# Last group of a hypergraph block kernel finished by graphs 0-1, 2 and 3; one store by halves; a shorter variance

## Chip, cores and metric

The kernel runs on one core of one Trainium2 chip. The metric is the device time of one launch in microseconds (us), the median of the runs shown. The engines are TensorE (PE in the profile, its weight loads PEld), VectorE (DVE), ScalarE (ACT), GpSimd (POOL) and SyncE (SP), which issues most of the transfers.

## Reference

64 independent graphs of 128 nodes with 256 features each. Per graph, with H = (adj != 0):

```
w    = adj[0, :]
Dinv = 1 / (H @ w)            Binv = 1 / column sums of H      (0 where the sum is 0)
conv(x, W, b) = Dinv * (H @ (Binv * (H^T @ (x @ W^T)))) + b
h    = relu(conv(x, W1, b1))                  # 128 x 512
h    = (h - mean) * rsqrt(var + 1e-5) * gamma + beta
y    = conv(h, W2, b2) + x                    # 128 x 256
out  = layernorm(x + y)                       # over the 256 features, eps 1e-5
```

## The kernel before

Four graphs make a group, 16 groups (0 to 15; LAST is 15). A = Dinv H Binv H^T is made once per graph and kept transposed (`at_sb`). For a group, in the names of the code:

- u = (A x) transposed, split into two parts `u_hi` and `u_lo` so that TensorE's faster type keeps the precision; v = W1 u in four chunks k of 128 hidden rows; `r_sb` = relu(v + b1) (ScalarE), `r_hi` a rounded copy (GpSimd, L894), `r_lo` the rest (VectorE, L661).
- The squares of r are added over the chunks (`pair_sb`, `q_sb`), turned by TensorE (`turned_q`, L318) and summed by ScalarE with an accumulating activation (L503) into `sum_sq`, one number a node.
- g = r W2 (scaled by gamma, centred) goes into `bank_g` (L301 to L308). `w2_hi` has two more columns than W2, filled with 1.0 (L919), so that column 256 of `bank_g` holds the sum of r. `make_var1` (L631 to L642) makes max(var, 0) + eps from that sum and `sum_sq`, for two graphs (a half) at a time; GpSimd raises it to -0.5 (`inverse_std1`, L870); `read_g` (L652) scales g by it and adds c2.
- y = A g (L325), `make_z` (L687) adds 2 x + b2 (from `xb_sb`, which GpSimd makes, L886), `take_stats2` and `make_var2` make mean and variance of z, GpSimd the power and the shift mean * rstd (`inverse_std2`, L901 and L909), ScalarE normalises in place (`normalise`, L493), SP stores the whole group (512 KB, L203).

Each engine has its own instruction stream, written out by hand, in which it waits on semaphores; nothing reorders it. A loop step i does on TensorE g of group i, v of i+1, y of i, and the preparation of later groups; on VectorE the statistics of group i-1, g of i, the splits of i+1.

The last group has no successor to interleave with. Its residual 2 x + b2 is put into PSUM by TensorE itself (`ident_2` times `xb_sb`, L427, all four graphs in a row), and y is accumulated on top (L431), a half at a time. Statistics are read straight from PSUM (L838). On VectorE its order is: statistics of group 14 graphs 0-1, variance of half 0, statistics of group 14 graphs 2-3, `read_g` half 0, variance of half 1, `make_var2(14)`, `read_g` half 1, then statistics and variance of z by halves. GpSimd does both `inverse_std1`, then `inverse_std2(14)`, then the two halves of `inverse_std2(15)`. ScalarE normalises group 14 and then graphs 0-1 of group 15 (L513, bias `last_shift2`), VectorE graphs 2-3 (L854). Each half is one store of 256 KB by SP.

Of the kernel before, what the change touches and what calls it, by code (L numbers as in the profile page):

```python
# [5 lines left out]
ALU = mybir.AluOpType  # L6
# [5 lines left out]
P = 128  # L12
# [7 lines left out]
def hypergraph_block(nc, x, adj, W1, b1, gamma, beta, W2, b2, out):  # L20
# [13 lines left out]
    with ExitStack() as ctx:  # L34
# [56 lines left out]
        stat1 = sb("stat1", [P, 4, PER])  # L91
# [9 lines left out]
        last_shift2 = sb("last_shift2", [P, PER // 2])  # L101
# [10 lines left out]
        SUM = DOUT  # L112
# [31 lines left out]
        out_ready, last_out_ready = sem("out_ready"), [sem("last_out_low"), sem("last_out_high")]  # L144
        last_shift2_ready = sem("last_shift2_ready")

# [18 lines left out]
        def _(sp):  # L165
# [31 lines left out]
            def store(i, half=None):  # L197
                part, n = graphs(half), len(each(half))
                if half is None:
                    sp.wait_ge(out_ready, i + 1)  # L200
                else:
                    sp.wait_ge(last_out_ready[half], 1)
                sp.dma_start(out_dram[:, i * PER + part.start:i * PER + part.start + n],  # L203
                             z_sb[:, i % 2, part]).then_inc(stored[i % 2], 16)
# [14 lines left out]
            for i in range(G):  # L219
# [9 lines left out]
                if i >= 1:  # L229
                    store(i - 1)  # L230
            for half in range(2):
                store(LAST, half)
            sp.wait_ge(stored[0], 16 * (G // 2))
            sp.wait_ge(stored[1], 16 * (G // 2) + 16)

        @block.tensor
        def _(pe):
# [57 lines left out]
            def make_g(i, n):  # L295
# [14 lines left out]
                if n % 2:  # L310
                    mm.then_inc(g_made, 1)

# [107 lines left out]
            for n in range(PER):  # L420
                if n < 2:
                    pe.wait_ge(z_ready, LAST * 2 - 1 + n)
                elif n == 2:
                    pe.wait_ge(at_ready, G)
                else:
                    pe.wait_ge(q_summed, G * 2)
                pe.matmul(last_z[n], ident_2[:, :], xb_sb[:, 1, n], start=True, stop=False)  # L427
            for half in range(2):
                pe.wait_ge(g_ready, LAST * 2 + half + 1)
                for n in each(half):  # L430
                    mm = pe.matmul(last_z[n], at_sb[:, LAST % 3, n], g_sb[:, n], start=False, stop=True)  # L431
                mm.then_inc(y_made, 1)

        @block.scalar
        def _(act):
# [54 lines left out]
            def normalise(i, half):  # L490
# [4 lines left out]
                if half:  # L495
                    ins.then_inc(out_ready, 1)

            def sum_q(i):
# [3 lines left out]
                for n in range(PER):  # L502
                    ins = nc.scalar.activation(scratch[:, n], turned_q[:, graph(n)], ACT.Copy,  # L503
# [4 lines left out]
            def normalise_last():  # L508

                act.wait_ge(last_shift2_ready, 1)  # L510
                act.wait_ge(stored[1], landed(LAST - 2, 2))
                for n in each(0):
                    ins = nc.scalar.activation(z_sb[:, 1, n], last_z[n], ACT.Identity,  # L513
                                               bias=last_shift2[:, n:n + 1], scale=rstd2[:, 1, n:n + 1])
                ins.then_inc(last_out_ready[0], 1)
# [75 lines left out]
        def _(dve):  # L591
# [387 lines left out]
```

## Time and profile before

| | us |
|---|---|
| median of 3 runs | 289.74 (289.73 to 290.66) |
| the profiled execution, its own time | 290.7 |
| its span in the trace | 288.9 |
| TensorE busy | 277.7 (96% of the span) |
| VectorE busy | 227.9 (79%) |
| ScalarE busy | 195.6 (68%) |
| GpSimd busy | 138.6 (48%) |

Times inside the kernel are counted from the span's start. The engines run side by side, so a busy share alone doesn't tell what sets the end; the chain of waits follows the work back from the last instruction. A busy time of TensorE contains the draining of its pipeline, so that consecutive matmuls overlap in the rows.

### The profile page before, as it was taken

Reading aid. Unit: us, or ns where it says so; the run is one execution under the profiler, and the core shown is the slowest. Engines: PE = TensorE matmul, PEld = TensorE weight load, DVE = VectorE, ACT = ScalarE, POOL = GpSimd, SP = SyncE. Lnnn points to the kernel's source line nnn. Section 1 sums busy time; section 2 is a strip of 40 time slices with the busy share of each in tenths; the row PEclk is TensorE's granted clock in tenths of the full one; section 3 lists DMA queues with packets and bytes.
Section 4 is the critical chain, followed back from the end, with each engine's and each line's share of the span. In section 5 each row is a group of like instructions: output and inputs, shape, how many; then the busy total and the mean of one; then the engine's idle time right before and its main releaser. Section 6 shows DMA issues by size and latency. Waiting matters only on the chain.

```text
span 288.9 us, 5778 instructions
## 1 busy us (share of the span) xinstructions
PE 277.7 (96%) x1814; PEld 249.0 (86%) x1814; DVE 227.9 (79%) x660; ACT 195.6 (68%) x556; POOL 138.6 (48%) x193
## 2 busy tenths in 40 slices
PE   6899999999999999999999999999999999999991
PEld 6779979898898989899898989899898989889880
DVE  1676579787979888797978888797988879596884
ACT  3288977766767876676677877676678775583614
POOL 2224463637364563636374463636365364536362
PEclk9999999999999999999999999999999999999998
DMA  7920140433513434431433533333423322120104
GB/s 218 309 79 19 40 127 16 112 113 63 173 41 122 113 94 115 122 114 54 152 70 93 140 99 109 100 104 53 136 50 91 97 88 75 36 73 2 50 25 145
DMA packets 37255, 27.70 MB, mean 96 GB/s; under 512 B 10013, under 2 KB 35305, under 8 KB 37225
## 3 DMA queue, kind: packets, MB, share of 16 engines
q1 hardware_dynamic: 37120, 27.30, 33.3%
q8 instruction: 14, 0.23, 0.3%
q14 instruction: 17, 0.13, 0.2%
q10 hardware_dynamic: 104, 0.04, 0.1%
HBM read 17.21 MB, written 8.42 MB: 89 GB/s over the span
## 4 chain that ended last, share of the span: by engine, by line
PE 85%; DVE 7%; issue 2%; POOL 2%; DMA 2%; ACT 1%; DVEq 0%; SPq 0%; POOLq 0%
PE bank_v L291 29%; PE bank_g L308 10%; PE bank_g L301 10%; PE bank_g L303 10%; PE bank_v L325 9%; PE bank_v L276 9%; PE bank_s L255 5%; PE bank_g L318 2%; DMA w_raw<-in_L_gnn_W_dram 2%; POOL rstd L870 1%; DVE g_sb L652 1%; DVE r_lo L661 1%; DVE pair_sb L666 1%; PE bank_g L333 1%; PE bank_g L353 1%
## 5 line engine op out<-in xcount | busy, mean ns | idle before, releaser
L886 POOL TENSOR_TENSOR xb_sb<-x_sb,b_half 128x512 f32<-128x512 f32 (+1 forms) x31 | 41.2, 1331 | 75.6 <-DVE r_lo L661 51.6
L481 ACT ACTIVATE r_sb<-bank_v,vec 128x512 f32<-128x512 f32 x64 | 44.2, 691 | 36.4 <-PE bank_v L291 35.7
L301 PE MATMUL bank_g<-w_hi,r_hi 128*128 128x258 f32 x256 | 65.5, 288 | 0.0
L303 PE MATMUL bank_g<-w_lo,r_hi 128*128 128x256 f32 x256 | 63.8, 282 | 0.0
L894 POOL TENSOR_SCALAR r_hi<-r_sb 128x512 fp32r<-128x512 f32 x64 | 47.9, 749 | 32.4 <-ACT r_sb L481 32.3
L661 DVE TENSOR_TENSOR r_lo<-r_sb,r_hi 128x512 fp32r<-128x512 f32 x64 | 44.7, 719 | 11.1 <-POOL r_hi L894 11.1
L291 PE MATMUL bank_v<-u_hi,w_hi 128*128 128x512 f32 x128 | 50.7, 396 | 0.4 <-DVE u_lo L625 0.4
L291 PE MATMUL bank_v<-u_hi,w_lo 128*128 128x512 f32 x128 | 50.8, 397 | 0.0
L291 PE MATMUL bank_v<-u_lo,w_hi 128*128 128x512 f32 x128 | 50.6, 395 | 0.0
L301 PEld LDWEIGHTS bank_g<-w_hi,r_hi 128*128 128x128 f32 x256 | 48.3, 189 | 1.4
L303 PEld LDWEIGHTS bank_g<-w_lo,r_hi 128*128 128x128 f32 x256 | 48.1, 188 | 1.2
L488 ACT ACTIVATE sq_sb<-r_sb 128x512 f32<-128x512 f32 x64 | 40.2, 634 | 1.9
L308 PE MATMUL bank_g<-w_hi,r_lo 128*128 128x258 f32 x256 | 41.3, 283 | 0.0
L475 ACT ACTIVATE u_hi<-bank_v 128x512 fp32r<-128x512 f32 x32 | 19.1, 598 | 27.0 <-PE bank_v L276 27.0
L493 ACT ACTIVATE z_sb<-z_sb,shift,rstd 128x256 f32<-128x256 f32 x60 | 32.3, 587 | 5.3 <-POOL shift L909 5.3
L308 PEld LDWEIGHTS bank_g<-w_hi,r_lo 128*128 128x128 f32 x256 | 35.2, 189 | 0.0
L870 POOL TENSOR_TENSOR rstd<-stat,half_power 128x2 f32<-128x2 f32 x32 | 22.7, 708 | 24.7 <-DVE stat L642 24.7
L652 DVE SCALAR_TENSOR_TENSOR g_sb<-bank_g,rstd,c 128x256 f32<-128x256 f32 x64 | 28.1, 481 | 8.0 <-POOL rstd L870 8.0
L276 PE MATMUL bank_v<-at_sb,x_sb 128*128 128x128 f32 x256 | 31.4, 276 | 0.7 <-ACT at_sb L469 0.7
L325 PE MATMUL bank_v<-g_sb,at_sb 128*128 128x256 f32 x120 | 31.9, 388 | 0.1
L276 PEld LDWEIGHTS bank_v<-at_sb,x_sb 128*128 128x128 f32 x256 | 29.8, 192 | 1.4 <-ACT at_sb L469 0.9
L325 PEld LDWEIGHTS bank_v<-g_sb,at_sb 128*128 128x128 f32 x120 | 21.4, 189 | 8.6 <-issue 5.3
(99 smaller groups left out, 449.1 us busy)
## 6 DMA issues: line engine op xcount, KB each, us to landing
x_sb<-in_x_dram SPq DMA_DIRECT2D x16, 512.0 KB, 3.8
out_dram<-z_sb SPq DMA_DIRECT2D x15, 512.0 KB, 3.2
adj_sb<-in_adj_dram SPq DMA_DIRECT2D x16, 256.0 KB, 4.0
d_row<-d_rows SPq DMA_DIRECT2D x13, 256.0 KB, 3.4
w_raw<-in_L_gnn_W_dram SPq DMA_DIRECT2D x2, 512.0 KB, 5.9
out_dram<-z_sb SPq DMA_DIRECT2D x2, 256.0 KB, 2.6
turned_h<-h_sb SPq DMA_TRANSPOSE x13, 2.4
d_rows<-dinv SPq DMA_DIRECT2D x13, 2.0 KB, 2.1
```

Of the source, the lines that this page charges most:

```text
L276: mm = pe.matmul(bank_v[:, c, graph(n)], x_sb[:, j % 3, n, graph(c)], at_sb[:, j % 3, n], start=True, stop=True)
L291: mm = pe.matmul(bank_v[:, k % 2], w[:, c, graph(k)], u[:, c], start=(m == 0), stop=(m == len(terms) - 1))
L301: pe.matmul(bank_g[:, n, 0:W2COLS], r_hi[:, i % 2, k, graph(n)], w2_hi[:, k], start=(k == 0), stop=False)
L303: pe.matmul(bank_g[:, n, 0:DOUT], r_hi[:, i % 2, k, graph(n)], w2_lo[:, k], start=False, stop=False, skip_group_check=True)
L308: mm = pe.matmul(bank_g[:, n, 0:W2COLS], r_lo[:, i % 2, k, graph(n)], w2_hi[:, k], start=False, stop=(k == KH - 1))
L325: mm = pe.matmul(bank_v[:, half, (n % 2) * DOUT:(n % 2 + 1) * DOUT], at_sb[:, i % 3, n], g_sb[:, n], start=True, stop=True)
L481: nc.scalar.activation(r_sb[:, k], bank_v[:, k % 2], ACT.Relu, bias=vec[:, k:k + 1]).then_inc(relu_ready, 1)
L488: nc.scalar.activation(sq_sb[:, k], r_sb[:, k], ACT.Square).then_inc(sq_ready, 1)
L493: ins = nc.scalar.activation(z_sb[:, i % 2, n], z_sb[:, i % 2, n], ACT.Identity, bias=shift2[:, n:n + 1], scale=rstd2[:, 0, n:n + 1])
L661: nc.vector.tensor_tensor(r_lo[:, i % 2, k], r_sb[:, k], r_hi[:, i % 2, k].bitcast(F32), ALU.subtract).then_inc(r_lo_ready, 1)
L886: nc.gpsimd.tensor_tensor(xb_sb[:, i % 2, part], x_sb[:, i % 3, part], b2_half[:, :].unsqueeze(1).to_broadcast([P, n, DOUT]), ALU.add).the ...
L894: nc.gpsimd.tensor_scalar(r_hi[:, i % 2, k], r_sb[:, k], 1.0, 1.0, ALU.mult, ALU.mult).then_inc(r_hi_ready, 1)
```

## The change

Five things are edited.

1. *Variance in three operations.* The two extra columns of `w2_hi` hold 1/512 and -1/512, so `bank_g` holds mean and -mean. ScalarE's sum of q is scaled by 1/512. For each graph one scalar_tensor_tensor makes mean * (-mean) + E[r^2], its scalar operand read from PSUM, and one tensor_scalar for the half does max and + eps. The wait for `q_summed` now stands ahead of the first operation. This holds in every group.
2. *Group 14 stored by halves:* ScalarE reports the first half (`half_out_ready`), and SP stores it before it waits for the second.
3. *Half 1 of group 15 graph by graph:* variance, power (GpSimd, one column each), `read_g` and y have signals of their own for graphs 2 and 3.
4. *Order in the last group.* VectorE: both statistics of group 14, variance of half 0, `make_var2(14)`, variance of graph 2, `read_g` half 0, variance of graph 3, `read_g` of 2 and of 3. GpSimd: `inverse_std1` of half 0, `inverse_std2(14)`, then the powers of graphs 2 and 3. TensorE: residual products of graphs 0-1, y of 0-1, residual products of 2-3, y of 2, y of 3.
5. *The last normalisation.* ScalarE does graphs 0-1 and then 2 (GpSimd makes the shift for both halves); VectorE does graph 3 alone. SP stores graphs 0-1 (256 KB) and graph 3 (128 KB); graph 2 (128 KB) is stored by a transfer that ScalarE issues itself.

```diff
+            sp.wait_ge(half_out_ready, 1)
+            store(LAST - 1, graphs(0))
+            sp.wait_ge(out_ready, LAST)
+            store(LAST - 1, graphs(1))
+            sp.wait_ge(last_out_ready[0], 1)
+            store(LAST, graphs(0))
+            sp.wait_ge(last_out_ready[2], 1)
+            store(LAST, slice(3, 4))
...
             for half in range(2):
-                pe.wait_ge(g_ready, LAST * 2 + half + 1)
                 for n in each(half):
+                    if n < 2:
+                        pe.wait_ge(z_ready, LAST * 2 - 1 + n)
+                    elif n == 2:
+                        pe.wait_ge(at_ready, G)
+                    else:
+                        pe.wait_ge(q_summed, G * 2)
+                    pe.matmul(last_z[n], ident_2[:, :], xb_sb[:, 1, n], start=True, stop=False)
+                for n in each(half):
+                    if half:
+                        pe.wait_ge(last_g_ready, n - 1)
+                    else:
+                        pe.wait_ge(g_ready, LAST * 2 + 1)
                     mm = pe.matmul(last_z[n], at_sb[:, LAST % 3, n], g_sb[:, n], start=False, stop=True)
...
-                    ins = nc.scalar.activation(scratch[:, n], turned_q[:, graph(n)], ACT.Copy,
+                    ins = nc.scalar.activation(scratch[:, n], turned_q[:, graph(n)], ACT.Copy, scale=1.0 / HID,
...
+                for part, graphs_done in enumerate((each(0), [2])):
+                    act.wait_ge(last_shift2_ready, part + 1)
+                    for n in graphs_done:
+                        ins = nc.scalar.activation(z_sb[:, 1, n], last_z[n], ACT.Identity,
+                                                   bias=last_shift2[:, n:n + 1], scale=rstd2[:, 1, n:n + 1])
+                    ins.then_inc(last_out_ready[part], 1)
+                act.wait_ge(last_out_ready[1], 1)
+                act.dma_start(out_dram[:, LAST * PER + 2:LAST * PER + 3], z_sb[:, 1, 2:3]).then_inc(stored[1], 16)
...
-                nc.vector.tensor_scalar(stat1[:, 0, part], bank_g[:, part, SUM], 1.0 / HID, None,
-                                        ALU.mult).then_inc(stat1_step, 1)
-                dve.wait_ge(stat1_step, done * 3 + 1)
-                nc.vector.tensor_tensor(stat1[:, 1, part], stat1[:, 0, part], stat1[:, 0, part],
-                                        ALU.mult).then_inc(stat1_step, 1)
                 dve.wait_ge(q_summed, done + 1)
-                dve.wait_ge(stat1_step, done * 3 + 2)
-                nc.vector.scalar_tensor_tensor(out=stat1[:, 2, part], in0=sum_sq[:, part], scalar=1.0 / HID,
-                                               in1=stat1[:, 1, part], op0=ALU.mult,
-                                               op1=ALU.subtract).then_inc(stat1_step, 1)
+                for n in each(half):
+                    ins = nc.vector.scalar_tensor_tensor(out=stat1[:, 0, n:n + 1], in0=bank_g[:, n, MEAN:MEAN + 1],
+                                                         scalar=bank_g[:, n, MEAN + 1:MEAN + 2],
+                                                         in1=sum_sq[:, n:n + 1], op0=ALU.mult, op1=ALU.add)
...
+            def make_last_var1(n):
+                dve.wait_ge(last_g_made if n == 2 else g_made, 1 if n == 2 else G * 2)
+                dve.wait_ge(q_summed, G * 2)
+                nc.vector.scalar_tensor_tensor(out=stat1[:, 0, n:n + 1], in0=bank_g[:, n, MEAN:MEAN + 1],
+                                               scalar=bank_g[:, n, MEAN + 1:MEAN + 2], in1=sum_sq[:, n:n + 1],
+                                               op0=ALU.mult, op1=ALU.add).then_inc(last_step, 1)
+                dve.wait_ge(last_step, n - 1)
+                nc.vector.tensor_scalar(stat1[:, 1, n:n + 1], stat1[:, 0, n:n + 1], 0.0, EPS, ALU.max,
+                                        ALU.add).then_inc(last_var1, 1)
+
+            def read_last_g(n):
+                dve.wait_ge(last_rstd1, n - 1)
+                nc.vector.scalar_tensor_tensor(out=g_sb[:, n], in0=bank_g[:, n, 0:DOUT], scalar=rstd1[:, n:n + 1],
+                                               in1=c2[:, :], op0=ALU.mult, op1=ALU.add).then_inc(last_g_ready, 1)
...
+            take_stats2(LAST - 1, 0)
+            take_stats2(LAST - 1, 1)
             make_var1(LAST, 0)
-            take_stats2(LAST - 1, 1)
+            make_var2(LAST - 1)
+            make_last_var1(2)
             read_g(LAST, 0)
-            make_var1(LAST, 1)
-            make_var2(LAST - 1)
-            read_g(LAST, 1)
-            take_last_stats2(0)
-            make_var2(LAST, 0)
-            take_last_stats2(1)
-            make_var2(LAST, 1)
+            make_last_var1(3)
+            read_last_g(2)
+            read_last_g(3)
+            for half in range(2):
+                take_last_stats2(half)
+                make_var2(LAST, half)
...
-            nc.gpsimd.memset(w2_hi[:, :, DOUT:W2COLS].bitcast(F32), 1.0)
+            for n, mean in enumerate((1.0 / HID, -1.0 / HID)):
+                nc.gpsimd.memset(w2_hi[:, :, DOUT + n:DOUT + n + 1].bitcast(F32), mean)
...
-            for half in range(2):
-                inverse_std1(LAST, half)
+            inverse_std1(LAST, 0)
             inverse_std2(LAST - 1)
+            for n in each(1):
+                pool.wait_ge(last_var1, n - 1)
+                nc.gpsimd.tensor_tensor(rstd1[:, n:n + 1], stat1[:, 1, n:n + 1], half_power[:, n:n + 1],
+                                        ALU.pow).then_inc(last_rstd1, 1)
```

## Rows read from the trace of the kernel before

**Rows 1.** Stretches: length, busy us (instructions) per engine, granted clock, DMA share, GB/s

```profile
200.00:250.00 50.00, 49.98 (x331) 45.08 (x330) 41.39 (x119) 33.48 (x91) 25.77 (x35) 1.00 0.30 85
```

**Rows 2.** Chain that ended last, in order of time: start, us, what

```profile
274.13 1.28 DVE z_sb L687 x2
...
284.16 0.71 POOL rstd L901
...
284.96 0.54 DVE z_sb L854
```

**Rows 3.** VectorE's timeline in the last group: start, us, operation, idle before

```profile
275.33 0.74 DVE L695 BATCH_NORM_STATS2 bn_sb<-z_sb 128x6 f32<-128x256 f32 x2
275.99 0.14 DVE L631 TENSOR_SCALAR stat<-bank_g 128x2 f32<-128x2 f32 x1
276.17 0.64 DVE L634 TENSOR_TENSOR stat<-stat 128x2 f32<-128x2 f32 x1
...
280.67 0.88 DVE L652 SCALAR_TENSOR_TENSOR g_sb<-bank_g,rstd,c 128x256 f32<-128x256 f32 x2 [0.32 <-POOL rstd L870]
281.46 0.75 DVE L838 BATCH_NORM_STATS2 bn_sb<-bank_v 128x6 f32<-128x256 f32 x2
...
282.52 0.17 DVE L708 TENSOR_SCALAR mean<-mv_sb 128x2 f32<-128x2 f32 x1
282.60 0.16 DVE L709 TENSOR_SCALAR var<-mv_sb 128x2 f32<-128x2 f32 x1
282.76 0.76 DVE L838 BATCH_NORM_STATS2 bn_sb<-bank_s 128x6 f32<-128x256 f32 x2
```

**Rows 4.** GpSimd's timeline in the last group

```profile
274.39 2.40 POOL L886 TENSOR_TENSOR xb_sb<-x_sb,b_half 128x1024 f32<-128x1024 f32 x1 [2.64 <-DVE q_sb L673]
...
279.87 0.70 POOL L870 TENSOR_TENSOR rstd<-stat,half_power 128x2 f32<-128x2 f32 x1 [1.80 <-DVE stat L642]
280.53 1.01 POOL L901 TENSOR_TENSOR rstd<-var,half_power 128x4 f32<-128x4 f32 x1
281.62 0.20 POOL L909 TENSOR_TENSOR shift<-mean,rstd 128x4 f32<-128x4 f32 x1
```

**Rows 5.** TensorE's timeline in the last group

```profile
279.00 1.03 PE L427 MATMUL bank_s<-xb_sb,ident 128*128 128x256 f32 x4
...
281.60 1.13 PE L431 MATMUL bank_s<-g_sb,at_sb 128*128 128x256 f32 x4 [0.70 <-DVE g_sb L652]
```

**Rows 6.** ScalarE's timeline in the last group

```profile
281.85 2.07 ACT L493 ACTIVATE z_sb<-z_sb,shift,rstd 128x256 f32<-128x256 f32 x4 [5.30 <-POOL shift L909]
```

**Rows 7.** SyncE's queue, first issue to the end of the last

```profile
283.95 2.41 SPq L203 DMA_DIRECT2D out_dram<-z_sb  x3
```

**Rows 8.** Stretches at the end, columns as in the first group

```profile
287.75:288.00 0.25, 0.00 (x0) 0.00 (x0) 0.00 (x0) 0.00 (x0) 0.00 (x0) 0.50 0.71 246
```

**Rows 9.** DMA issues in the last 3 us: size, us to landing

```profile
out_dram<-z_sb SPq DMA_DIRECT2D x1, 256.0 KB, 2.4
```

**Rows 10.** DMA issues of the whole run, ScalarE's queue

```profile
edge_rows<-in_adj_dram ACTq DMA_DIRECT2D x1, 32.0 KB, 3.2
```

**Rows 11.** VectorE's timeline in group 14's second half

```profile
267.33 0.16 DVE L631 TENSOR_SCALAR stat<-bank_g 128x2 f32<-128x2 f32 x1 [1.47 <-PE bank_g L308]
...
267.80 0.16 DVE L638 SCALAR_TENSOR_TENSOR stat<-sum_sq,stat 128x2 f32<-128x2 f32 x1
267.99 0.17 DVE L642 TENSOR_SCALAR stat<-stat 128x2 f32<-128x2 f32 x1
...
269.85 0.82 DVE L661 TENSOR_TENSOR r_lo<-r_sb,r_hi 128x512 fp32r<-128x512 f32 x1
```

**Rows 12.** GpSimd's timeline in group 14's second half

```profile
269.51 0.63 POOL L894 TENSOR_SCALAR r_hi<-r_sb 128x512 fp32r<-128x512 f32 x1 [0.55 <-ACT r_sb L481]
...
270.90 0.85 POOL L894 TENSOR_SCALAR r_hi<-r_sb 128x512 fp32r<-128x512 f32 x1 [0.76 <-ACT r_sb L481]
```

**Rows 13.** TensorE's timeline, first use of the fourth chunk in group 15

```profile
272.61 0.28 PE L301 MATMUL bank_g<-w_hi,r_hi 128*128 128x258 f32 x1
```

More of the change, by code:

```diff
@@ L195, in load_d, with store @@
                     [P, P * PER])).then_inc(d_row_in[j % 2], 16)
[L197 to L203, printed above, removed]
+            def store(i, part=slice(0, PER)):
+                sp.dma_start(out_dram[:, i * PER + part.start:i * PER + part.stop],
                              z_sb[:, i % 2, part]).then_inc(stored[i % 2], 16)
@@ L228, in _ @@
                     load_x(i + 3)
-                if i >= 1:
+                if 1 <= i < LAST:
+                    sp.wait_ge(out_ready, i)
                     store(i - 1)
-            for half in range(2):
-                store(LAST, half)
-            sp.wait_ge(stored[0], 16 * (G // 2))
-            sp.wait_ge(stored[1], 16 * (G // 2) + 16)
+            sp.wait_ge(half_out_ready, 1)
[6 more added lines that the diff above has]
+            store(LAST, slice(3, 4))
+            sp.wait_ge(stored[0], 16 * (G // 2) + 16)
+            sp.wait_ge(stored[1], 16 * (G // 2) + 32)
         @block.tensor
@@ L311, in make_g @@
                     mm.then_inc(g_made, 1)
+                elif i == LAST and n == 2:
+                    mm.then_inc(last_g_made, 1)
             def turn_q(i):
@@ L419, in _ @@
             pe.wait_ge(xb_ready, G * 2)
[L420 to L427, printed above, removed]
             for half in range(2):
-                pe.wait_ge(g_ready, LAST * 2 + half + 1)
                 for n in each(half):
+                    if n < 2:
[10 more added lines that the diff above has]
+                        pe.wait_ge(g_ready, LAST * 2 + 1)
                     mm = pe.matmul(last_z[n], at_sb[:, LAST % 3, n], g_sb[:, n], start=False, stop=True)
-                mm.then_inc(y_made, 1)
+                    if half:
+                        mm.then_inc(last_y_made, 1)
+                if half == 0:
+                    mm.then_inc(y_made, 1)
         @block.scalar
@@ L496, in normalise @@
                     ins.then_inc(out_ready, 1)
+                elif i == LAST - 1:
+                    ins.then_inc(half_out_ready, 1)
             def sum_q(i):
@@ L845, in _ @@
-            make_var2(LAST - 1)
-            read_g(LAST, 1)
-            take_last_stats2(0)
-            make_var2(LAST, 0)
-            take_last_stats2(1)
-            make_var2(LAST, 1)
+            make_last_var1(3)
[4 more added lines that the diff above has]
+                make_var2(LAST, half)
             dve.wait_ge(stored[1], landed(LAST - 2, 2))
             dve.wait_ge(rstd2_ready, G + 1)
-            for n in each(1):
-                ins = nc.vector.tensor_scalar(z_sb[:, 1, n], last_z[n], mean2[:, 1, n:n + 1],
-                                              rstd2[:, 1, n:n + 1], ALU.add, ALU.mult)
@@ L856, in _ @@
-            ins.then_inc(last_out_ready[1], 1)
+            nc.vector.tensor_scalar(z_sb[:, 1, 3], last_z[3], mean2[:, 1, 3:4], rstd2[:, 1, 3:4], ALU.add,
+                                    ALU.mult).then_inc(last_out_ready[2], 1)
         @block.gpsimd
@@ L869, in inverse_std1 @@
                 pool.wait_ge(var1_ready, i * 2 + half + 1)
-                nc.gpsimd.tensor_tensor(rstd1[:, part], stat1[:, 3, part], half_power[:, part],
+                nc.gpsimd.tensor_tensor(rstd1[:, part], stat1[:, 1, part], half_power[:, part],
                                         ALU.pow).then_inc(rstd1_ready, 1)
@@ L903, in inverse_std2 @@
                 pool.wait_ge(rstd2_ready, done + 1)
-                if half == 0:
-                    nc.gpsimd.tensor_tensor(last_shift2[:, :], mean2[:, 1, part], rstd2[:, 1, part],
+                if half is not None:
+                    nc.gpsimd.tensor_tensor(last_shift2[:, part], mean2[:, 1, part], rstd2[:, 1, part],
                                             ALU.mult).then_inc(last_shift2_ready, 1)
-                if half is not None:
                     return
```

26 lines of the change are left out of this document (12 added, 14 removed).

## Prediction

> **What bounds the kernel now.** I read the table of stretches first. Over 200 to 250 us TensorE is busy 49.98 of 50 us at a granted clock of 1.00 [rows 1], so the loop over groups is TensorE's. VectorE has 8.6 us idle in the same stretch, and nothing that only shortens VectorE's share of a loop step can shorten the step. Nearly the whole change lies behind the loop, in the last 15 us.
>
> I read the chain of waits next. From 274.13 on it has no TensorE piece: it goes over VectorE's z of group 14, statistics, the small variance operations, GpSimd's power, g, statistics, power, and the last normalisation [rows 2]. Then I went down each engine's timeline over the last 14 us [rows 3 to 7]: VectorE and GpSimd hand the work to and fro, and every other engine waits for them. The table of stretches at the end shows the DMA engines 71% busy between 287.75 and 288.00 at 246 GB/s [rows 8]: a full rate of 246 / 0.71 = 346 GB/s, and the last bytes leave at about 287.93. Three stores (512 + 256 + 256 KB = 1.05 MB) at that rate take 3.03 us, so they began at 284.90, 0.95 after group 14's store was issued at 283.95. The last store was issued at 283.95 + 2.41 - 0.37 = 285.99 [rows 7] and took 2.4 us to land [rows 9], so 288.39: 0.46 after its last byte, and 0.5 before the span's end. The end is thus set by the compute chain and, to a smaller part, by a backlog of stores.
>
> **The variance in three operations.** Before, a half takes four dependent operations, in group 14's second half from 267.33 to 267.99 + 0.17 = 268.16, 0.83 [rows 11]. After, two scalar_tensor_tensors that don't wait for each other (0.08 apart, as the two rows of mean and variance at 282.52 and 282.60 show for independent small operations [rows 3]) and one tensor_scalar 0.19 behind (267.80 to 267.99 [rows 11]), 0.17 long: 0.44. That is 0.39 us less in each half. In the loop it is covered by TensorE and I cost it at nothing. Could it leak into the end through group 14? Behind it VectorE runs dense, but its r_lo at 269.85 takes 0.82, with GpSimd's r_hi running since 269.51, where z at 274.13, also over 512 columns, takes 0.64 [rows 2, 11, 12]; 0.39 earlier VectorE would be at 269.46, in a dead heat with it, and the two would only swap places, since GpSimd waits there for ScalarE and that for TensorE. I take 0, with 0.2 of gain as the other end. The scalar operand now comes from PSUM: no row shows that. The nearest are a small operation reading PSUM (0.14 at 275.99) [rows 3] and one reading only SBUF (0.16 at 267.80) [rows 11]; I take 0.16, with 0.1 more each as the upper end, 0.2 in all on the path. ScalarE's factor in the sum of q rides in an operation that exists: 0. The second memset on GpSimd, some 0.1 us, lies in the set-up while GpSimd waits for ScalarE: 0.
>
> **Group 15's first half.** Before, two statistics of group 14 (275.33) end with the next start at 275.99, so 0.66 a pair; then the squaring at 276.17 takes 0.64 instead of some 0.16, until 276.81, which is where GpSimd's add of b2 ends (274.39 + 2.40 = 276.79) [rows 3, 4]. The variance of group 15's first half then still needs two operations. After, both pairs come first: 275.33 + 0.66 + 0.66 = 276.65. Then 0.08, 0.19 and 0.17: ready at 277.09, the power 0.08 later, 277.17 to 277.88 (0.71 [rows 2]). Before, the squaring's end at 276.81 with the 0.17 and 0.19 of two more operations, 0.08 between each, puts it at about 277.4; so it comes some 0.2 earlier although a pair of statistics was moved ahead of it. The squaring, two SBUF inputs, is gone; the new operation reads PSUM, PSUM and SBUF, like z at 274.13 (both in 1.28), which ran beside the same add [rows 2]. If it is held up until 276.79 anyway, 0.14 is lost.
> The Trainium skill ("SBUF — State Buffer", Who interferes with whom) says that a VectorE instruction with two SBUF inputs contends with a GpSimd instruction that reads SBUF, and one with a single SBUF input doesn't; by that rule the 0.14 doesn't arise, and the trace's 0.64 agrees with it.
>
> **The order behind it.** make_var2(14), moved ahead of read_g, starts at 277.00. For two graphs such a block takes 0.56 behind the statistics (282.76 + 0.76 to 284.16 - 0.08 [rows 2, 3]); two more aggregates of 0.16 at most make 0.88 at most, so 277.88 or sooner, when GpSimd comes free. It starts a waiting power 0.04 before the end of the one before (279.87 + 0.70, 280.53 [rows 4]), so that of group 14 runs 277.84 to 278.85 (1.01), the shift 278.93 to 279.13 (0.08 and 0.20, as 281.54 to 281.82 before) [rows 4]. It was ready at 281.82 before. Queued behind both is now the power of graph 2; its variance is wanted only by 279.09 and is ready long before, since on TensorE graph 3's g and two residual pairs still come behind graph 2's g, and the second of these pairs starts at 279.00 [rows 5]. A power of one column isn't in the trace: two columns take 0.71, four 1.01, so 0.15 a column and 0.56 for one; bounds 0.20 (the shift) and 0.71. With starts 0.04 before an end as above: graph 2 279.09 to 279.65, graph 3 279.61 to 280.17 (its variance is ready at 279.2, after read_g of graphs 0 and 1, 277.99 to 278.87). VectorE's g of graph 3 starts 0.10 later (280.57 to 280.67 before [rows 3, 4]), at 280.27. Before, a pair started at 280.67 and the statistics 0.79 later, 0.40 a graph; now one graph is left, and they start at 280.67, not 281.46.
>
> **TensorE's products.** Before, the residual products of graphs 2 and 3 start at 279.00 and take 1.03 [rows 5]. After, y of graphs 0 and 1 takes that place (its g is ready at 278.87) and ends at 280.03. The residuals of 2 and 3 come then, 1.03 at most (a next pair may start before the last has drained), to 281.06, and y of 2 and 3 in 1.13 as before (281.60), to 282.19 at the latest, graph 2 by 281.7. Statistics of graph 0 want 280.03 and start at 280.67, those of graph 2 are due at 281.89 and of graph 3 at 282.27: the work hides all of it, the last by 0.08 at the worst.
>
> **The end.** Statistics to the variance's start: 281.46 to 282.60, then 0.08: the second pair starts at 280.67 + 1.22 = 281.89. Before it had to wait for y until 282.73 (281.60 + 1.13 [rows 5]). From its start to the power is 1.40 (282.76 to 284.16 [rows 2, 3]): 283.29, end 284.00 (0.71). VectorE normalises graph 3 0.80 after the power's start, as 284.16 to 284.96 [rows 2], at 284.09, and is done in 0.54: 284.63, store issued at 284.67. ScalarE normalises graph 2 after the new shift (0.08 + 0.20) and 0.03 more (281.82 to 281.85 [rows 4, 6]), at 284.31; one graph takes 2.07 less three times 0.5, 0.57: 284.88; its own DMA is issued 0.04 later, at 284.92. ScalarE is free: group 14's four run from 279.16 to 281.23 (2.07 [rows 6]), the first half's two from 283.05 to 284.07.
> Group 14's stores are issued at about 280.3 and 281.3 and have left before 283.1. Group 15's: 256 KB issued at 284.10, then 128 KB at 284.67 and 128 KB at 284.92. Together 524 kB at 346 GB/s from 285.05: 286.57, and 0.46 to landing: 287.03. Alone, the last one would land at 284.92 + 0.95 + 0.38 + 0.46 = 286.71, so the backlog still sets it, by 0.32. Landing was at 288.39: **1.36 us gained**. Of this, 1.07 is the last issue (285.99 to 284.92), 0.29 the smaller backlog.
> ScalarE's queue is unused from the start until then. Its only larger transfer took 3.2 us for 32 KB, while SP's queue was loading [rows 10]. The nearest row is SP's last store, so I take the sum above; with 3.2 it lands at 288.12 and 1.1 of the gain is gone.
> The Trainium skill ("DMA: Bandwidth & Descriptors", Where the ~2 µs actually goes) speaks against cutting a store: each pays about 2.0 us fixed, mostly for the receipt. By it the last piece lands near 284.92 + 2.0 + 0.3 = 287.2, and the sum would be 1.2. This trace's 0.95 ahead of the bytes and 0.46 behind make 1.41 instead.
>
> **The sum.** The profiled execution spans 288.9 and took 290.7, 1.8 outside the span; I leave those alone. 290.7 - 1.36 = 289.3, or -0.47%. The median of three runs is 289.74, 0.96 below the profiled one; the same difference gives 288.4. About 0.5% (1.45 us) is what a measurement of this kernel can tell from no change, and the sum lies just under it.
>
> **The rivals.**
> *More than the sum:* the 0.39 does leak through group 14, or the one-column power is nearer 0.45. For it: after 269.5 VectorE is dense. Against: the tie with GpSimd's r_hi [rows 12]. Another 0.2: 288.2.
> *The new small operations are dear:* a power of one column costs 0.71 as two do (0.30 over the two), PSUM scalars 0.2. All on the path: gain 0.9, 288.85.
> *ScalarE's queue is slow to wake:* 3.2 us to landing [rows 10]; gain 0.27, 289.5, no change. For it: the only row of that queue. Against: those engines were full with SP's loads.
> *Slower:* VectorE's earlier instructions in the loop take the memory access from GpSimd before r_hi of the fourth chunk. It ends at 271.75 (270.90 + 0.85) and TensorE first wants it at 272.61 [rows 12, 13], so it has 0.86 to spare. A single VectorE operation (0.64) in its way costs nothing; from 0.86 on it decides, and two in its way cost about 0.4 in each of 14 groups, 5.6 us less 1.4: 294. Against: VectorE moves by 0.39 only, and GpSimd's turn still comes when ScalarE releases it.
>
> **How the numbers follow.** The forecast has 0.62, with its own range 288.0 to 288.8 (0.15 lost at the start, 0.15 a power, 0.2 either way for joints between engines). More than the sum 0.14, dear operations 0.08, the sleeping queue 0.10, slower 0.06. Two in ten left out over both ends: 287.9 to 289.4. Faster by over 0.5% means below 288.29: nearly all of the first rival and 0.28 of the forecast's 0.62, 0.41. Slower by over 0.5%: 0.06. Within: 0.53.
>
> **What the profile after would show.** The step right: first power of group 15 at 277.2, its one-column powers 0.56 long, g of graph 3 at 280.3, second statistics at 281.9, last store issued at 284.9 by ScalarE's queue, landing at 287.0; loop steps unchanged at TensorE. Wrong, if the loop's TensorE idles, if one-column powers take 0.7, if scalar_tensor_tensor with a PSUM scalar is over 0.25, or if ScalarE's store takes over 2.4 us to land.

## The result and the profile after

The changed kernel takes 288.02 us (median of 4 runs, 288.00 to 288.05) against 289.74: a ratio of 0.9933, 95% interval 0.9914 to 0.9952, 1.72 us. The forecast was 1.36 us, with "within 0.5%" as the likeliest outcome (0.53). The profiled executions stand 2.65 us apart (290.7 and 288.05; spans 288.9 and 286.2), because that of before lies about 0.95 above the kernel's median; the first experiment accounts for this.

The last group after the change, from VectorE's timeline:

```profile
274.00 1.40 DVE L709 BATCH_NORM_STATS2 bn_sb<-z_sb 128x6 f32<-128x256 f32 x4
275.31 0.34 DVE L651 SCALAR_TENSOR_TENSOR stat<-bank_g,sum_sq 128x1 f32<-128x1 f32 x2
275.69 0.17 DVE L656 TENSOR_SCALAR stat<-stat 128x2 f32<-128x2 f32 x1
...
277.10 0.88 DVE L666 SCALAR_TENSOR_TENSOR g_sb<-bank_g,rstd,c 128x256 f32<-128x256 f32 x2 [0.36 <-issue]
...
278.43 1.02 DVE L857 SCALAR_TENSOR_TENSOR g_sb<-bank_g,rstd,c 128x256 f32<-128x256 f32 x2
279.36 0.75 DVE L867 BATCH_NORM_STATS2 bn_sb<-bank_v 128x6 f32<-128x256 f32 x2
...
280.58 0.78 DVE L867 BATCH_NORM_STATS2 bn_sb<-bank_s 128x6 f32<-128x256 f32 x2
...
282.80 0.54 DVE L884 TENSOR_SCALAR z_sb<-bank_s,mean,rstd 128x256 f32<-128x256 f32 x1 [0.89 <-POOL rstd L930]
```

GpSimd's timeline in the same stretch:

```profile
275.93 0.71 POOL L899 TENSOR_TENSOR rstd<-stat,half_power 128x2 f32<-128x2 f32 x1 [0.48 <-DVE stat L656]
276.61 1.01 POOL L930 TENSOR_TENSOR rstd<-var,half_power 128x4 f32<-128x4 f32 x1
277.70 0.20 POOL L937 TENSOR_TENSOR shift<-mean,rstd 128x4 f32<-128x4 f32 x1
277.85 1.08 POOL L985 TENSOR_TENSOR rstd<-stat,half_power 128x1 f32<-128x1 f32 x2
...
281.99 0.70 POOL L930 TENSOR_TENSOR rstd<-var,half_power 128x2 f32<-128x2 f32 x1 [0.27 <-DVE var L723]
```

TensorE's timeline, and then ScalarE's with its own store:

```profile
276.83 1.02 PE L435 MATMUL bank_v<-xb_sb,ident 128*128 128x256 f32 x4
278.03 1.13 PE L441 MATMUL bank_v<-g_sb,at_sb 128*128 128x256 f32 x4 [0.18 <-DVE g_sb L666]
279.00 1.03 PE L435 MATMUL bank_s<-xb_sb,ident 128*128 128x256 f32 x4
279.86 1.03 PE L441 MATMUL bank_s<-g_sb,at_sb 128*128 128x256 f32 x4
```

```profile
283.00 0.56 ACT L529 ACTIVATE z_sb<-bank_s,last_shift,rstd 128x256 f32<-128x256 f32 x1 [0.16 <-POOL last_shift L934]
283.59 0.39 ACTq L533 DMA_DIRECT2D out_dram<-z_sb  x1
```

The DMA issues of the last 8 us, with the time to landing:

```profile
out_dram<-z_sb SPq DMA_DIRECT2D x3, 256.0 KB, 2.2
out_dram<-z_sb SPq DMA_DIRECT2D x1, 128.0 KB, 2.0
out_dram<-z_sb ACTq DMA_DIRECT2D x1, 128.0 KB, 2.2
```

The first residual product marks the end of the loop in both traces. In the kernel before it starts at 278.14, the 0.86 of one pair ahead of the 279.00 of [rows 5]; in the changed kernel it starts at 276.83. So the work up to that point came 1.31 earlier, and 1.31 has to be added to a time of the changed kernel to compare it with the prediction's:

| step | predicted | measured + 1.31 |
|---|---|---|
| first power of group 15 | 277.17 | 277.24 |
| end of the one-column powers | 280.17 | 280.24 |
| statistics of graph 0 | 280.67 | 280.67 |
| statistics of graph 2 | 281.89 | 281.89 |
| last power | 283.29 | 283.30 |
| graph 3 normalised from | 284.09 | 284.11 |
| ScalarE's store issued | 284.92 | 284.90 |
| end of the span | 287.54 | 287.5 |

In these terms the sum behind the loop holds to 0.1 us. What it lacks lies ahead of the first residual product. TensorE starts y of the first half of groups 0, 1 and 2 at 40.11, 56.91 and 73.32 in the kernel before, steps of 16.80 and 16.41, and at 39.19, 55.57 and 71.98 in the changed kernel, steps of 16.38 and 16.41. One step, that from group 0 to group 1, is 0.42 shorter; all later ones up to group 14 are equal to 0.01. A table in the trace of the kernel before points at the cause. It lists which engine waited for whom (us in total, times, longest); these are TensorE's weight loads:

```profile
PEld bank_s L431 <- DVE g_sb L652: 1.1, 1, 1.1
PEld bank_v L325 <- DVE g_sb L652: 0.5, 1, 0.5
```

The first line is the last group. The second is y of group 0, second half: once in the run, TensorE waits for VectorE's g inside the loop. After the change that line is gone.

### The profile page after: what moved, and what is told of

The parts are those of the page before. It is cut to its first block, busy times and chain, and to the rows that moved or that the text cites. A ratio compares the mean times of both kernels' runs of the same rounds, so it can differ in the third digit from the quotient of the medians.

```text
span 286.2 us, 5751 instructions
## 1 busy us (share of the span) xinstructions
PE 275.8 (96%) x1814; PEld 247.5 (86%) x1814; DVE 227.0 (79%) x628; ACT 196.1 (69%) x557; POOL 136.0 (47%) x196
## 4 chain that ended last, share of the span: by engine, by line
PE 89%; DVE 5%; POOL 2%; issue 2%; ACT 1%; POOLq 0%; DVEq 0%
PE bank_v L296 30%; PE bank_g L313 10%; PE bank_g L306 10%; PE bank_g L308 10%; PE bank_v L332 10%; PE bank_v L281 9%; PE bank_s L260 5%; PE bank_g L325 2%; PE bank_s L365 1%; DVE pair_sb L680 1%; DVE r_lo L675 1%; PE bank_g L360 1%; POOL rstd L930 1%; PE bank_s L267 1%; DVE bn_sb L867 1%
## 5 line engine op out<-in xcount | busy, mean ns | idle before, releaser
L923 POOL TENSOR_SCALAR r_hi<-r_sb 128x512 fp32r<-128x512 f32 x64 | 44.8, 699 | 41.3 <-ACT r_sb L494 41.3
L675 DVE TENSOR_TENSOR r_lo<-r_sb,r_hi 128x512 fp32r<-128x512 f32 x64 | 48.4, 776 | 11.3 <-POOL r_hi L923 11.3
L666 DVE SCALAR_TENSOR_TENSOR g_sb<-bank_g,rstd,c 128x256 f32<-128x256 f32 x62 | 27.1, 478 | 7.3 <-POOL rstd L899 6.9
L899 POOL TENSOR_TENSOR rstd<-stat,half_power 128x2 f32<-128x2 f32 x31 | 21.9, 708 | 17.4 <-DVE stat L656 17.3
L296 PEld LDWEIGHTS bank_v<-u_lo,w_hi 128*128 128x128 f32 x128 | 24.0, 188 | 5.5
```

The lines of the kernel that those rows point to most:

```text
L296: mm = pe.matmul(bank_v[:, k % 2], w[:, c, graph(k)], u[:, c], start=(m == 0), stop=(m == len(terms) - 1))
L675: nc.vector.tensor_tensor(r_lo[:, i % 2, k], r_sb[:, k], r_hi[:, i % 2, k].bitcast(F32), ALU.subtract).then_inc(r_lo_ready, 1)
L923: nc.gpsimd.tensor_scalar(r_hi[:, i % 2, k], r_sb[:, k], 1.0, 1.0, ALU.mult, ALU.mult).then_inc(r_hi_ready, 1)
```

## Experiments

All times are medians, and the ratios are against the kernel before, which was run beside them and gave 289.71 to 289.74.

**1. The kernel before once more.** No edit.

> The kernel before, unchanged, for a second profile. The theory: 0.94 us of the two shown spans (288.9 and 286.2) is no work of the change but of the one profiled execution of before, whose W1 transposes and first S products ran at 0.43 us a matmul where after shows 0.28; this profile should show about 0.28, a span of 288.0, and still a wait of TensorE of 0.4 to 0.5 for g of group 0's second half (the line that makes y waits for VectorE's g). The rival, that the shorter set-up belongs to the change: the W1 transposes take 0.43 again and the span is 288.9.

289.74 us (one run), span 287.9. TensorE's transposes of W1 in the trace behind the recorded rows, and then in this one (min/median/max ns, first and last start):

```profile
L333 PE MATMUL bank_g<-ident,w_raw x8: 421/421/475, 6.0 to 7.6; 128*128 128x128 f32 x8
```

```profile
L333 PE MATMUL bank_g<-ident,w_raw x8: 272/273/331, 6.4 to 7.2; 128*128 128x128 f32 x8
```

W1 arrived later here (6.4), and yet u of group 0 starts at 12.04 and not at 12.96: 0.92 us of the difference between the two profiled executions was one execution's set-up and belongs to no edit. The other 0.4 of the 1.31 is still there between this kernel and the changed one (y of groups 0 and 1 at 39.18 and 55.97, a step of 16.79), and so does TensorE's wait for g.

Group 0 around it, VectorE's timeline of this kernel and then of the changed one:

```profile
35.67 0.88 DVE L652 SCALAR_TENSOR_TENSOR g_sb<-bank_g,rstd,c 128x256 f32<-128x256 f32 x2 [0.92 <-POOL rstd L870]
...
37.40 0.15 DVE L631 TENSOR_SCALAR stat<-bank_g 128x2 f32<-128x2 f32 x1
37.59 0.38 DVE L634 TENSOR_TENSOR stat<-stat 128x2 f32<-128x2 f32 x1
38.08 0.16 DVE L638 SCALAR_TENSOR_TENSOR stat<-sum_sq,stat 128x2 f32<-128x2 f32 x1
38.28 0.17 DVE L642 TENSOR_SCALAR stat<-stat 128x2 f32<-128x2 f32 x1
39.35 0.88 DVE L652 SCALAR_TENSOR_TENSOR g_sb<-bank_g,rstd,c 128x256 f32<-128x256 f32 x2 [0.90 <-POOL rstd L870]
```

```profile
35.44 0.88 DVE L666 SCALAR_TENSOR_TENSOR g_sb<-bank_g,rstd,c 128x256 f32<-128x256 f32 x2 [0.91 <-POOL rstd L899]
...
37.17 0.35 DVE L651 SCALAR_TENSOR_TENSOR stat<-bank_g,sum_sq 128x1 f32<-128x1 f32 x2
37.55 0.21 DVE L656 TENSOR_SCALAR stat<-stat 128x2 f32<-128x2 f32 x1
38.66 0.88 DVE L666 SCALAR_TENSOR_TENSOR g_sb<-bank_g,rstd,c 128x256 f32<-128x256 f32 x2 [0.90 <-POOL rstd L899]
```

Up to 33.9 VectorE runs alike in both. The first half's shorter variance brings g forward by 0.23, the second's by another 0.46, of which 0.2 is the squaring: 0.38 long here instead of 0.16, while GpSimd's r_hi ran from 37.04 to 37.97. TensorE, which starts y of the first half at 39.18 and needs 0.86 for it, could begin the second at 40.04 and begins at 40.28; S behind it then starts 0.34 and u 0.41 later than in the changed kernel.

**2. The shorter variance alone, in all groups.** The kernel before with the first part of the change (columns, scaled sum and operations as there); order, split and stores stay.

```diff
-                nc.vector.tensor_scalar(stat1[:, 0, part], bank_g[:, part, SUM], 1.0 / HID, None,
-                                        ALU.mult).then_inc(stat1_step, 1)
...
+                for n in each(half):
+                    ins = nc.vector.scalar_tensor_tensor(out=stat1[:, 0, n:n + 1], in0=bank_g[:, n, MEAN:MEAN + 1],
+                                                         scalar=bank_g[:, n, MEAN + 1:MEAN + 2],
+                                                         in1=sum_sq[:, n:n + 1], op0=ALU.mult, op1=ALU.add)
```

> Before, with only the three-operation variance (all groups, with the scaled columns and the scaled sum). Theory A: TensorE's wait in group 0 goes (0.42 us), and in the last group the first power comes 0.7 earlier, of which about 0.6 reaches the end because the residual products then hold y of the first half until 280.9: 1.0 us faster than before, 288.7. Rival B, the recorded forecast (the shorter variance is worth nothing in the loop, 0.2 at the start of the end): 289.5. The steps of the loop from group 1 on keep 16.41 us by either.

288.76 us, ratio 0.9967 [0.9947, 0.9986]: 0.98 faster. The step from group 0 to 1 is 16.38, as in the changed kernel. In the last group, VectorE's and TensorE's timelines show the second part; the first residual product is at 278.13, so the times can be held against before as they are:

```profile
276.14 0.35 DVE L633 SCALAR_TENSOR_TENSOR stat<-bank_g,sum_sq 128x1 f32<-128x1 f32 x2
...
279.92 0.88 DVE L648 SCALAR_TENSOR_TENSOR g_sb<-bank_g,rstd,c 128x256 f32<-128x256 f32 x2
280.92 0.76 DVE L834 BATCH_NORM_STATS2 bn_sb<-bank_v 128x6 f32<-128x256 f32 x2
```

```profile
279.86 1.03 PE L431 MATMUL bank_v<-g_sb,at_sb 128*128 128x256 f32 x4
```

The first power of the group starts 0.47 earlier (276.88 against 277.35), not the 0.7 of theory A. g of the second half starts 0.75 earlier than in [rows 3], but the statistics only 0.54, since y of the first half, behind four residual products, ends at 280.89. Theory A holds in both places and in the total; rival B, the forecast's own view of the loop, is out.

**3. Three operations in one half only: group 0, second.** All other halves keep four (on the scaled columns).

```diff
             def make_var1(i, half):
                 part, done = graphs(half), i * 2 + half
                 dve.wait_ge(g_made, done + 1)
+                if i == 0 and half == 1:
+                    dve.wait_ge(q_summed, done + 1)
+                    for n in each(half):
...
+                else:
+                    stat1_inc(nc.vector.tensor_scalar(stat1[:, 2, part], bank_g[:, part, MEAN], 1.0, None, ALU.mult))
...
```

> Before, with three operations in one place only, group 0's second half; all other halves keep four (the scaled columns and the scaled sum stay, at the same number of operations). Theory A: the whole loop gain sits there: 0.42 us faster, 289.3, and no wait of TensorE for g in group 0. Rival B: the gain is spread over the loop or comes through group 14: 0.0 to 0.05 us.

289.57 us, 0.17 faster, ratio 0.9993 [0.9977, 1.001]; the interval alone doesn't tell it from nothing, but the step from group 0 to 1 does: 16.62 against 16.79 (y at 39.18 and 55.80). Theory A said 0.42: a miss. TensorE's wait for g is gone as expected, and another stands in its place:

```profile
PE bank_v L276 <- DVE z_sb L702: 0.2, 1, 0.2
```

The first chunk of u needs z of group 0's first half, which VectorE makes behind g, r_lo and a pair sum: at 41.32 here, at 41.08 in the changed kernel, where the first half's shorter variance had brought all of this forward. The gain of 0.42 needs both halves of group 0.

**4. The changed kernel with four operations in that one half.** The same edit on the changed kernel, its condition turned round.

> The changed kernel, with four operations in group 0's second half only. Theory A: it gives back 0.42 us against the changed kernel (288.4 instead of 288.0), the wait of TensorE for g of group 0 is back, and the end behind the loop is as long as in the changed kernel. Rival B: 288.0.

288.37 us, ratio 0.9947 [0.9931, 0.9964]: 0.35 of the 0.42 come back. The step is 16.70, with a wait of 0.2 for g and one of 0.15 for z. The end keeps its length: the statistics of graph 0 start 2.54 behind the first residual product, against 2.53 in the changed kernel. With the second half short (experiment 3) the step gives 0.17, with the first 0.09, with both 0.41: two waits, one behind the other, so that removing one uncovers the other.

**5. The changed kernel with four operations in every half of `make_var1`.** The same edit with a condition that never holds; `make_last_var1` stays.

> The changed kernel with four dependent operations in every half that make_var1 handles (groups 0 to 14 and the first half of group 15), keeping the new order, the split of the last half, and the stores. Theory A (the sum in parts): 0.41 us come back in group 0, and in the last group the first variance is 0.27 later than in the changed kernel, which GpSimd's queue of powers hands on whole: 0.7 slower than the changed kernel, 288.7, so that order, split and stores alone are worth 1.0 of the 1.7. Rival B (the recorded forecast's tail: 1.36 belongs to the order, split and stores, the loop to nothing): 288.4.

288.71 us, ratio 0.9975 [0.9963, 0.9988], 0.69 above the changed kernel. The new order, split and stores give 1.03, the shorter variance alone 0.98 (experiment 2), both together 1.72, so 0.29 is counted twice. Two things overlap. This run keeps the short variance of graphs 2 and 3. And VectorE's timeline shows the squaring of the first half with four operations:

```profile
275.87 0.16 DVE L668 TENSOR_TENSOR stat<-stat 128x2 f32<-128x2 f32 x1
```

It took 0.64 in [rows 3]. Behind both pairs of statistics it starts when GpSimd's add of b2 has ended (273.44 + 2.40 = 275.84), so the new order avoids that stall without the shorter variance. How the 0.29 divides between the two wasn't tested.

**6. All four residual products first.**

```diff
+            for n in range(PER):
...
+                pe.matmul(last_z[n], ident_2[:, :], xb_sb[:, 1, n], start=True, stop=False)
             for half in range(2):
-                for n in each(half):
...
-                    pe.matmul(last_z[n], ident_2[:, :], xb_sb[:, 1, n], start=True, stop=False)
                 for n in each(half):
```

> The changed kernel with all four residual products ahead of y, as before the change. Theory A: y of graphs 0 and 1 starts 0.5 later (0.86 of products ahead of it, 0.34 of which it would have waited for g anyway), its end at about 279.6 passes the statistics' start at 279.36, and 0.2 to 0.25 reaches the end: 288.25. Rival C: the chain over GpSimd's powers and g of graph 3 covers it: 288.0.

288.24 us, ratio 0.9957 [0.9945, 0.9969], 0.22 above the changed kernel. TensorE:

```profile
277.49 1.03 PE L434 MATMUL bank_s<-xb_sb,ident 128*128 128x256 f32 x4
278.35 1.03 PE L441 MATMUL bank_v<-g_sb,at_sb 128*128 128x256 f32 x4
```

y ends at 279.38 and the statistics start at 279.42, 2.79 behind the first residual product (276.63) instead of 2.53 (276.83 to 279.36). Theory A; putting the residual products in two places is worth 0.2.

**7. Graph 2 stored by SP.**

```diff
+            sp.wait_ge(last_out_ready[1], 1)
+            store(LAST, slice(2, 3))
...
-                act.wait_ge(last_out_ready[1], 1)
-                act.dma_start(out_dram[:, LAST * PER + 2:LAST * PER + 3], z_sb[:, 1, 2:3]).then_inc(stored[1], 16)
```

> The changed kernel, with the store of graph 2 issued by SP behind that of graph 3, nothing by ScalarE. Theory A (the store on ScalarE's queue only saves the issue): SP's issue of graph 3 runs from 283.38 to 283.75, the one of graph 2 behind it is 0.15 to 0.2 later than ScalarE's, but the bytes still queue behind those of graph 3: at most 0.15 slower, 288.0 to 288.15. Rival D (ScalarE's queue lands late, from the recorded prediction): faster than the changed kernel.

288.03 us, ratio 0.9959 [0.9947, 0.9971]. Its runs form two levels, six at 287.9 to 288.0 and five at 288.9 to 289.8 (the difference that experiment 10 is about), and the median is of the lower: no difference to the changed kernel, as theory A allows. In its trace the last issue begins 6.99 behind the first residual product (284.61 and 277.62), in the changed kernel 6.76, but it lands in 2.0 instead of 2.2. ScalarE's queue, unused for 280 us, was thus not slow to land: 2.2 us, and the rival with 3.2 is out.

**8. S between the halves of y.** In a step of the loop the chain of waits shows a first half of y of 0.86 and a second of 1.10, here in the changed kernel:

```profile
88.55 0.86 PE bank_v L332 x4
89.42 0.01 issue
89.42 1.10 PE bank_v L332 x4
90.53 0.89 PE bank_s L260 x8
```

```diff
                 make_y(i, 0)
-                make_y(i, 1)
                 if i + 3 < G:
                     make_s(i + 3)
+                make_y(i, 1)
...
                     make_z(i, 0)
-                    make_z(i, 1)
                     add_pair(i + 1, 1)
+                    make_z(i, 1)
```

> The changed kernel with TensorE's loop order y half 0, S of group i+3, y half 1 (before: y, y, S), and VectorE's pair sum between the two z. Theory E: each of 14 steps has a gap of 0.24 us between the two halves of y, in which TensorE waits for ScalarE's relu of the fourth chunk (the chain shows 0.86 for the first four matmuls and 1.10 for the second); S fills it in 12 steps: 2.9 us faster at best, 285.1. Rival F: z of the second half then comes too late for the second chunk of u, or q too late for its transposes, and the wait only moves: 288 or more.

288.13 us, ratio 0.9937 [0.9923, 0.9952], no better than the changed kernel. Its six runs spread from 286.97, the profiled one, to 288.40, and four lie a microsecond or more above the profiled one; what delays those isn't shown. The chain in the same place:

```profile
88.39 0.86 PE bank_v L332 x4
89.25 0.89 PE bank_s L260 x8
90.14 0.86 PE bank_v L332 x4
91.00 1.94 PE bank_v L281 x16
```

The second half of y falls to 0.86: the gap was a wait. For what, no row names (the table of waits puts fourteen such waits down to "issue"). In the code it waits for ScalarE's relu of the next group's fourth chunk, which ends at 89.28 in the changed kernel. But u grows from 1.78 to 1.94. In the code its second chunk waits for z of the second half, which now starts at 91.04 and not at 90.56. In the profiled run the step is 16.32 or 16.33 instead of 16.41; twelve of them make 1.0 us, which the median doesn't show. By the median it is rival F.

**9. Group 14 stored whole.**

```diff
-            sp.wait_ge(half_out_ready, 1)
-            store(LAST - 1, graphs(0))
             sp.wait_ge(out_ready, LAST)
-            store(LAST - 1, graphs(1))
+            store(LAST - 1)
...
-            sp.wait_ge(stored[0], 16 * (G // 2) + 16)
+            sp.wait_ge(stored[0], 16 * (G // 2))
```

> The changed kernel with group 14 stored in one piece behind its second half. Theory: group 14 is normalised at 280.0 in the changed kernel, so even its whole store has left by 282.5, over a microsecond before the first bytes of group 15: no difference, 288.0. Rival (the recorded prediction's second term, 0.3 us less backlog, is earned by the halves): 288.2 to 288.3.

288.00 us, ratio 0.9938 [0.9919, 0.9957], span 286.2: no difference. Storing by halves earns nothing. Group 14's whole store is issued at 280.02 and lands in 3.0 us, about when the first store of group 15 is issued, so what keeps the backlog small is that group 14 is normalised earlier.

**10. TensorE kept busy while it waits for W1.**

```diff
+KEEP_WARM = 8
...
             pe.transpose(bank_v[:, 1, 0:N], edge_rows[:, :], ident[0:N, 0:N]).then_inc(edges_turned, 1)
+            for _ in range(KEEP_WARM):
+                pe.transpose(bank_q[:, :].bitcast(BF16)[:, graph(0)], ident_b[:, :], ident_b[:, :])
```

> The changed kernel with eight more idle-time transposes of the identity on TensorE between the edge rows and W1's transposes, which fill the 0.2 to 1.1 us in which it waits for W1. Theory: the runs at about 289.0 are those in which the clock was still at its lower level at W1's transposes and the first S products; without the idle time before them all runs come at one level, 288.0 to 288.2. Rival: TensorE's idle time there has no part in it; both levels remain, and 0.2 to 0.4 us are lost where W1 arrives early.

288.01 us, ratio 0.9932 [0.9915, 0.9949], six runs from 287.94 to 288.04. Without it some runs of most kernels lie about 0.9 or more higher (5 of 11 in experiment 7, 1 of 6 in experiment 9), here none. The edit costs nothing. Whether it helps isn't shown: of 129 runs of the kernel before and of experiments 2 to 7 and 9, 27 lie 0.7 us or more above their median, about one in five. By chance alone, six runs without one would then come in one try out of four.

**11. S in halves.** As experiment 8, with S of graphs 0-1 ahead of the second half of y and S of graphs 2-3 behind it. VectorE's pair sum stays between the two z as there.

```diff
-            def make_s(j):
+            def make_s(j, half=None):
...
-                for n in range(PER):
+                for n in each(half):
...
-                mm.then_inc(s_made, 1)
+                if half != 0:
+                    mm.then_inc(s_made, 1)
...
                 make_y(i, 0)
+                if i + 3 < G:
+                    make_s(i + 3, 0)
                 make_y(i, 1)
                 if i + 3 < G:
-                    make_s(i + 3)
+                    make_s(i + 3, 1)
```

> The changed kernel with S of group i+3 cut in two on TensorE: y half 0, S of graphs 0-1, y half 1, S of graphs 2-3, u. The version with the whole S in between shortened a step from 16.41 to 16.32 us, because the second chunk of u then waited for VectorE's z. Theory E: with only half of S in front, y half 1 still finds its bank read by ScalarE and z has 0.44 us more: the step falls to 16.17, 12 steps save 2.9 us, 285.1. Rival F: the wait moves on to r_lo or q's transposes: a step of over 16.3.

285.13 us, four runs within 0.02, ratio 0.9833 [0.9814, 0.9852]: 4.6 us faster than before and 2.9 faster than the changed kernel. The chain:

```profile
88.26 0.86 PE bank_v L333 x4
89.12 0.44 PE bank_s L260 x4
89.56 0.87 PE bank_v L333 x4
90.43 0.44 PE bank_s L260 x4
90.87 1.79 PE bank_v L282 x16
```

Neither y nor u is stretched. The step is 16.17 (y of groups 2 and 3 at 71.93 and 88.10), 0.24 shorter, twelve times, which makes the 2.9. Theory E. In group 0 it isn't free: there the first half of S takes 0.68 instead of 0.44, and the step is 16.60, so about half of the 0.42 is lost again; the last step of the loop is 0.12 shorter. VectorE's pair sum was moved in the same edit and wasn't tried alone.

**12. The edits of experiments 10 and 11 together.**

> The two edits of the runs before together: S in halves and the eight idle-time transposes. Theory: they add, 285.2, without runs at the upper level. Rival: as for the two alone.

285.12 us, ratio 0.9833 [0.9813, 0.9852]. The same as experiment 11, none of whose four runs lay higher either, so this says nothing on the eight transposes.

## Why the prediction was wrong

*The time.* 288.02 lies in the range of 287.9 to 289.4, but 1.72 us (0.67% by the ratio) is more than the 1.36 forecast and falls on the other side of 0.5%. That it also lies just inside the forecast's own range, 288.0 to 288.8, is luck: that range allows for joints between engines at the end, and the missing 0.42 is at the start.

*The step that failed* is the one that reads "In the loop it is covered by TensorE and I cost it at nothing". It was concluded from one stretch, 200 to 250 us, in which TensorE is busy throughout. That holds from group 1 to group 14, where no step moved by more than 0.01. It doesn't hold for group 0, in which TensorE waited for VectorE's g. That group has another order in the code (u of group 1 and S of group 2 come between its g); whether this is why VectorE is late there wasn't tested. Experiments 1 to 4 show the gain from both sides: 0.42 us, in that step alone, and only with both halves shortened. The leak considered, through group 14, gave nothing: VectorE's statistics of group 14 start 1.33 earlier (275.33 and 274.00), the residual products 1.31.

*The last group* was right in all terms of the table above, and with it the forecast mechanism: VectorE and GpSimd hand over to each other, and TensorE's products stay hidden. 1.36 and 0.42 make 1.78 against 1.72 measured. One step that the table doesn't have was off. g of graphs 0-1 was to start at 277.99 and started at 277.10 + 1.31 = 278.41, behind 0.36 of idle time that the profile puts down to "issue", although its power had ended at 276.64. That took up most of the slack of y of graphs 0-1 (ready at 280.47 instead of 280.03, wanted at 280.67) and of graph 3's variance. It cost nothing: in experiment 4 the idle time is absent, and the end is as long. Its cause isn't known.

*Single prices.* A power of one column: 0.56 expected, 0.55 measured. The small operation with its scalar in PSUM: 0.16 expected, 0.21 to 0.22 measured; a half's variance takes 0.55 (275.31 to 275.86), not 0.44, so it saves 0.28 and not 0.39. This stayed within the bound of 0.1 and cost the 0.07 by which the first power came late; the slack behind it (the hand-over from the powers to g) took it up. GpSimd's add of b2 doesn't hold up the new operation. In the changed kernel it had all but ended (275.46), but in experiment 2 it lasted until 276.78, and the two new operations at 276.14 took 0.35 beside it, as long as elsewhere. The tensor_scalar behind them, at 276.52, took 0.28 there instead of 0.17, until 276.80; in group 0 of the changed kernel it took 0.21, until 37.76, with GpSimd's r_hi ending at 37.74. Both end with GpSimd's operation, so one SBUF input seems not to keep every operation of VectorE clear of GpSimd, as the prediction has it. No run tested this alone.

*The stores.* ScalarE's store landed in 2.2 us, at 287.1 on the prediction's scale. That rules out the 3.2 of [rows 10], but lies between the sum's 287.03 and the 287.2 of 2.0 fixed plus 0.3; SP's 128 KB landed in 2.0, less than those 2.3. Of the separate ideas in the change, the halves of group 14 (experiment 9) and ScalarE's issue (experiment 7) earn nothing measurable, the two places of the residual products 0.2. The single graph per engine in the last normalisation wasn't tried alone; its 0.45 is argued from [rows 2] and [rows 3].

*The sizes of the rivals.* "More than the sum" had 0.14 and named the wrong place. The slower rival (GpSimd's r_hi pushed back) didn't occur: from group 1 to group 14 the steps are equal to 0.01.

*The profiled execution* of the kernel before was 0.95 above its median. The prediction rightly carried that over unchanged, but it could have asked where those 0.95 lie: experiment 1 puts 0.92 of them into the set-up.

## What to carry to other kernels

A loop that is bound by one engine in the middle need not be so in its first steps. Read the bound engine's waits over the whole run, down to those that occur only once, before a saving on another engine is costed at nothing. Where two waits lie one behind the other, removing one shows only part of the gain: here 0.17 and 0.09 alone, 0.41 together. And where a bound engine's group of equal instructions is longer in one place than in another (1.10 beside 0.86), there can be a wait in it that "busy" hides. Here 0.44 us of independent work filled the gap of 0.24, while 0.89 made another wait out of it.

## What the hardware showed beyond that

TensorE's eight transposes of W1 took 421 ns each in one execution and 272 in another of the same code, and the eight products of S behind them 1.99 and 1.16 us; from u on the two run in parallel, 0.92 us apart. The cause is open. The granted clock reads 1.00 in that stretch both times, which is the upper of its two levels (2.4 GHz), and 421 to 272 is a factor of 1.55, not the 2 between the levels. Nor does TensorE's idle time ahead of the transposes sort the executions: it was 0.59, 0.50 and 1.09 us where they took 417 to 421 (the kernel before, experiments 7 and 2) and 0.41 and 0.92 where they took 272 (the changed kernel, experiment 1).

VectorE's small operation on one column took 0.21 us with its scalar operand in PSUM (median of 62), against 0.16 with two columns and the tensor operands in SBUF.
